# One more gate/up group ahead: TensorE's order in a fused cross-attention and mixture-of-experts kernel, lead of three against lead of four

## The chip, the cores and the metric

The kernel runs on one core of one Trainium2 chip. The metric is device time in microseconds (us); three runs of the kernel before stand below, and one further execution was profiled.

## The reference

Input `x` is 4 x 1024 tokens of width 256 in fp32, `ctx_1024` is 4 x 154 context rows of the same width.

```
x = x + attention(layernorm(x), ctx, ctx)        # one head, keys masked, softmax over 154 keys
xn = layernorm(x)                                # 4096 tokens
combine = top-8-of-16 routing weights of xn      # sigmoid scores, normalised, zero elsewhere
g, u = xn @ w_gate[e], xn @ w_up[e]              # 256 -> 128, for each of 16 experts
y[e] = (silu(g) * u) @ w_down[e]                 # 128 -> 256
x = x + sum_e combine[e] * y[e] + shared expert  # the shared one is expert 0 of the kernel's 17
```

## The kernel before

The 4096 tokens go in eight chunks of 512. For each chunk all 17 experts (`NE = 17`, numbered 0 to 16, number 0 the shared one) are computed, with all weights resident in SBUF as a high and a low part, so that each product is three matmuls. Chunks are indexed `(b, hf)`; a hardware loop `pe.Fori(0, B - 1)` of three turns holds two chunks per turn, and the last two chunks stand behind it. Every engine has its own copy of this loop.

One expert of one chunk takes these steps, each by the engine named:

- `gate_up(e)`, TensorE: six matmuls of 512 columns into `gate_ps[i]`, then six into `up_ps[i]`. There are two PSUM banks of each, `i` alternating from expert to expert.
- `tanh_gate(e)`, ScalarE (L666): tanh of the gate bank into `ew[i]`.
- `silu_up(e)`, VectorE: L949 combines tanh and the gate bank and signals `silu_done`; L953 multiplies by the up bank and signals `prod_done`.
- `weighted(e)`, GpSimd (L1160, L1153 for expert 0): times the token's routing weight, into `h[i]`.
- `hidden_hi(e)`, ScalarE (L673), and `hidden_lo(e)`, VectorE (L959): the high and low parts `hs[i]`. `hidden_hi(e)` waits for `down_done` of expert e - 2, whose `hs` it overwrites.
- `down(e)`, TensorE: twelve matmuls of 256 columns that accumulate into `y_ps`.

TensorE's order is written out by hand in `chunk`: at step s it issues `down(s)`, then pieces of work for the next chunk that are due at s (`front(s)`), then `gate_up(s + 3)`, then the pieces due at s + .5. `gate_up(e)` waits for `silu_done` of expert e - 2 ahead of its first matmul (its gate bank was read for the last time), and for `prod_done` of expert e - 2 ahead of its seventh. Numbers past 16 are experts of the next chunk, written 0', 1' and so on below.

The pieces for the next chunk are placed by tables. On TensorE: `turn_x` 2.5, `scores` 4.5 and 5.5, `turn_p` 7.5, `attend` 8.5, `turn_ln2` 11.5 (transposes of the second layernorm's output, L386, into `f_ps`), `logits` 12.5, `turn_z` 13, `turn_c` 15. VectorE's order at step s is `silu_up(s + 2)`, front(s), `hidden_lo(s + 1)`, front(s + .5); ScalarE's is `tanh_gate(s + 2)`, front(s), `hidden_hi(s + 1)`, front(s + .5); GpSimd's is `weighted(s + 1)`, front(s + .5). VectorE has at 9.5 the residual (L900), the statistics of the second layernorm (L823, L829), at 10.5 its scaling (L836), at 11.5 the low parts of its transposes (L854, after ScalarE's L617). All four engines take their instructions in this order and none is skipped over a wait.

Ahead of the loop TensorE runs the attention and routing of the first chunk, then `gate_up` 0, 1 and 2, while ScalarE and VectorE split the staged weights (`split_w`, L613 and L818).

Of the kernel before, what the change touches and what calls it, by code (L numbers as in the profile page):

```python
# [50 lines left out]
def xattn_moe_kernel(nc, x, ctx, mask, Wq, bq, Wk, bk, Wv, bv, gate_w, w_gate, w_up, w_down,  # L51
                     sw_gate, sw_up, sw_down, out):
    B, S, D = x.shape
    KEYS = ctx.shape[1]
    E, _, H = w_gate.shape
    TOK = 512
    TILES = TOK // P
    CHUNKS = B * S // TOK
    KD = D // P
    NE = E + 1  # L60
# [18 lines left out]
    with ExitStack() as stack:  # L79
# [101 lines left out]


        FREE = 2

        def upto(b, hf, per, k):

            return b * (2 * per) + (per * hf + k)

        def first_chunk(b, hf):
            return isinstance(b, int) and b == 0 and hf == 0  # L190

        def wait_apart(eng, *waits):


            counts = [n if isinstance(n, int) else eng.to_reg(n) for _, n in waits]
            eng.wait_ge(consts_set, 1)
            for (what, _), n in zip(waits, counts):
                eng.wait_ge(what, n)
# [5 lines left out]
        def slot(hf, e):  # L204

            return (NE * hf + e) % 2

        def nxt(hf, e):

            return (hf, e) if e < NE else (hf + 1, e - NE)  # L210
# [5 lines left out]
        def _(sp):  # L216
            sp.sem_inc(stored, 16 * FREE)
            sp.dma_start(ctx_in[:, 0:CT - 1, :], ctx_rows[0:(CT - 1) * P, :].rearrange("(t p) d -> p t d", p=P)) \
# [28 lines left out]
            def spread(b, hf, pair):  # L247

                stored_c = (c_stored, upto(b, hf, 16, 16))
                if pair >= PLACES:  # L250
                    wait_apart(sp, (h_done, upto(b, hf, NE, 2 * (pair - PLACES) + 3 + FREE)))
                elif first_chunk(b, hf):
                    wait_apart(sp, stored_c)
                else:
                    wait_apart(sp, (h_done, upto(b, hf - 1, NE, 2 * (pair + PLACES) + 3 + FREE)), stored_c)
                sp.dma_start(cb[:, pair % PLACES].rearrange("p a t -> p (a t)"),
                             c_rows[2 * pair:2 * pair + 2, :].rearrange("a t -> (a t)").partition_broadcast(P)) \
                    .then_inc(cb_loaded[pair % PLACES], 16)
# [4 lines left out]
            def chunk(b, hf, load):  # L263
# [5 lines left out]
                for pair in range(PLACES):  # L269
                    spread(b, hf + 1, pair)  # L270
                sp.wait_ge(y_added, upto(b, hf, 2, 2 + FREE))
                sp.dma_start(out_rows[b * 2 + hf], x2[:, hf]).then_inc(stored, 16)

            def last_stores():

                for q in range(2):
                    sp.wait_ge(y_added, 2 * CHUNKS + FREE - 1 + q)
                    sp.dma_start(out_rows[CHUNKS - 1, :, 2 * q:2 * q + 2, :], x2[:, 1, 2 * q:2 * q + 2, :]) \
                        .then_inc(stored, 16)
# [7 lines left out]
            last_stores()  # L287
            sp.wait_ge(stored, 16 * (CHUNKS + 1 + FREE))


        @block.tensor
        def _(pe):
            mm = nc.tensor.matmul

            def three_pass(ps, pairs, first, last):

                for i, ((lh, ll), (rh, rl)) in enumerate(pairs):
                    mm(ps, lh, rh, start=first and i == 0, stop=False)  # L298
                    mm(ps, lh, rl, start=False, stop=False)  # L299
                    ins = mm(ps, ll, rh, start=False, stop=last and i == len(pairs) - 1)  # L300
                return ins
# [151 lines left out]
            def turn_c(b, hf):  # L453
                pe.wait_ge(combined, upto(b, hf, 1, 1))
                for j in range(TILES):
                    ins = nc.tensor.transpose(f_ps[1][0:E, j * P:(j + 1) * P], cw[:, j, :], ident[:])
                ins.then_inc(c_turned, 1)

            def gate_up(b, hf, e):
                hf, e = nxt(hf, e)  # L460
                i, par = slot(hf, e), hf % 2
                if e == 0:
                    pe.wait_ge(t2_hi, upto(b, hf, 2, 2))
                    pe.wait_ge(t2_lo, upto(b, hf, 2, 2))
                if hf == 0:
                    pe.wait_ge(w_hi, e + 1)
                    pe.wait_ge(w_lo, e + 1)
                for ps, col, free, done in ((gate_ps, 0, silu_done, gate_done), (up_ps, UP0, prod_done, up_done)):
                    pe.wait_ge(free, upto(b, hf, NE, e - 1 + FREE))
                    ins = three_pass(ps[i][:], [((W[:, e, HI, col + k * H:col + (k + 1) * H],  # L470
                                                  W[:, e, LO, col + k * H:col + (k + 1) * H]),
                                                 (xT[:, par, HI, k, :], xT[:, par, LO, k, :])) for k in range(KD)],
                                     first=True, last=True)
                    ins.then_inc(done, 1)

            def down(b, hf, e):
                i = slot(hf, e)
                pe.wait_ge(h_hi, upto(b, hf, NE, e + 1 + FREE))
                pe.wait_ge(h_lo, upto(b, hf, NE, e + 1 + FREE))
                if e == 0:  # L480
                    pe.wait_ge(y_added, upto(b, hf, 2, FREE))
                for j in range(TILES):


                    c = slice(j * P, (j + 1) * P)
                    ins = three_pass(y_ps[j // 2][:, (j % 2) * D:(j % 2 + 1) * D],
                                     [((hs[:, i, HI, c], hs[:, i, LO, c]),
                                       (W[:, e, HI, DN0:DN0 + D], W[:, e, LO, DN0:DN0 + D]))],
                                     first=e == 0 and j % 2 == 0, last=e == NE - 1 and j % 2 == 1)
                    if e == NE - 1 and j == 1:  # L490
                        ins.then_inc(y_half, 1)
                ins.then_inc(down_done, 1)

            def front(at, b, hf):

                for part in due(PE_AT, "turn_x", at):
                    turn_x(b, hf, part)
                for part in due(PE_AT, "scores", at):
                    scores(b, hf, part)
                for part in due(PE_AT, "turn_p", at):  # L500
                    turn_p(b, hf, part)
                for part in due(PE_AT, "attend", at):
                    attend(b, hf, part)
                for part in due(PE_AT, "turn_ln2", at):
                    turn_ln2(b, hf, part)
                if due(PE_AT, "logits", at):
                    logits(b, hf)
                if due(PE_AT, "turn_z", at):
                    turn_z(b, hf)
                if due(PE_AT, "turn_c", at):  # L510
                    turn_c(b, hf)

            def chunk(b, hf, ahead, last):
                for s in range(NE):
                    down(b, hf, s)
                    if ahead:
                        front(s, b, hf + 1)
                    if s + 3 < NE or not last:
                        gate_up(b, hf, s + 3)
                    if ahead:  # L520
                        front(s + .5, b, hf + 1)

# [27 lines left out]
            pe.wait_ge(v_lo, 2 * B)  # L550
            gate_up(0, 0, 0)
            turn_c(0, 0)
            gate_up(0, 0, 1)
            gate_up(0, 0, 2)
            with pe.Fori(0, B - 1) as b:
                chunk(b, 0, True, False)
                chunk(b, 1, True, False)
            chunk(B - 1, 0, True, False)
            chunk(B - 1, 1, False, True)

# [658 lines left out]
```

## Time and profile before

| | us |
|---|---|
| three runs | 711.46, 715.76, 718.47 |
| median | 715.76 |
| span of the profiled execution | 717.8 |
| TensorE matmul busy in that span | 691.6 |
| VectorE, ScalarE, GpSimd busy | 459.2, 239.8, 260.7 |

The span runs from the first to the last instruction of the profiled execution. Nothing else was recorded of that execution's time: its span is 2.0 above the median of the three runs and inside their range. The page names TensorE "PE", VectorE "DVE", ScalarE "ACT", GpSimd "POOL". A matmul row's duration reaches past the start of the next one, since matmuls are pipelined, so the pace is read from starts.

### The profile page before, as it was taken

How to read it: one execution, taken by the hardware profiler on the slowest of the kernel's cores; microseconds unless marked ns; L12 is line 12 of the kernel's file. 1: busy time of each engine (PE TensorE's matmuls, PEld its weight loads, DVE VectorE, ACT ScalarE, POOL GpSimd, SP SyncE). 2: the span in 40 equal slices, each digit the busy share in tenths (PEclk: the TensorE clock that was granted, in tenths of full speed). 3: DMA queues.
4: the chain of work that ended last, by engine and by line, in shares of the span. 5: the costliest groups of instructions: out<-in, count | busy, mean ns of one | idle time of the engine just before them, and what ended most of it. 6: DMA issues, size and time to landing. Idle time of an engine off the chain costs nothing.

```text
span 717.8 us, 11775 instructions
## 1 busy us (share of the span) xinstructions
PE 691.6 (96%) x3995; PEld 595.8 (83%) x3995; DVE 459.2 (64%) x1029; ACT 239.8 (33%) x485; POOL 260.7 (36%) x222
## 2 busy tenths in 40 slices
PE   7997799999999899999999899999999999999997
PEld 6575688888888788888888788888988888888886
DVE  4576666677667475777566576677565775775444
ACT  4345233333424134233333234242334233232221
POOL 2120432535343242435344243434324343433432
PEclk9799999999999899999999999999999999999999
DMA  6315511032110510005100411005110421006100
GB/s 184 111 32 162 184 60 46 13 103 106 59 31 1 180 60 30 30 24 185 59 30 1 151 59 60 30 2 192 46 58 0 136 94 38 1 3 204 61 0 31
DMA packets 32772, 51.30 MB, mean 71 GB/s; under 512 B 3918, under 2 KB 24391, under 8 KB 32711
## 3 DMA queue, kind: packets, MB, share of 16 engines
q1 hardware_dynamic: 32455, 50.23, 21.6%
q8 instruction: 37, 0.61, 0.4%
q10 hardware_dynamic: 256, 0.26, 0.2%
q14 instruction: 24, 0.20, 0.1%
HBM read 46.03 MB, written 4.46 MB: 70 GB/s over the span
## 4 chain that ended last, share of the span: by engine, by line
PE 91%; issue 4%; DVE 2%; POOL 1%; ACT 1%; DMA 1%; POOLq 0%; SPq 0%; DVEq 0%; ACTq 0%
PE y_ps L298 9%; PE y_ps L300 9%; PE y_ps L299 9%; PE gate_ps L298 9%; PE up_ps L298 9%; PE gate_ps L300 9%; PE gate_ps L299 8%; PE up_ps L300 8%; PE up_ps L299 8%; PE f_ps L386 2%; PE f_ps L408 2%; PE f_ps L419 1%; PE up_ps L368 1%; PE up_ps L307 1%; DMA xin<-in_x_dram 1%
## 5 line engine op out<-in xcount | busy, mean ns | idle before, releaser
L1160 POOL TENSOR_TENSOR hidden<-hidden,cb 128x512 f32<-128x512 f32 x128 | 200.1, 1565 | 308.2 <-DVE hidden L953 257.4
L949 DVE SCALAR_TENSOR_TENSOR hidden<-hidden,gate_ps 128x512 f32<-128x512 f32 x136 | 93.2, 685 | 156.2 <-ACT hidden L666 145.9
L666 ACT ACTIVATE hidden<-gate_ps 128x512 f32<-128x512 f32 x136 | 81.5, 599 | 275.0 <-PE gate_ps L300 273.4
L298 PE MATMUL y_ps<-W,hs 128*128 128x256 f32 x544 | 157.9, 290 | 13.4 <-issue 5.7
L300 PE MATMUL y_ps<-W,hs 128*128 128x256 f32 x544 | 154.8, 284 | 0.0
L299 PE MATMUL y_ps<-W,hs 128*128 128x256 f32 x544 | 154.5, 284 | 0.0
L298 PEld LDWEIGHTS y_ps<-W,hs 128*128 128x128 f32 x544 | 103.8, 191 | 19.9 <-issue 9.5
L959 DVE TENSOR_TENSOR hs<-hidden,hs 128x512 fp32r<-128x512 f32 x136 | 95.6, 703 | 29.1 <-ACT hs L673 29.1
L298 PE MATMUL gate_ps<-xT,W 128*128 128x512 f32 x272 | 109.1, 401 | 0.0
L298 PE MATMUL up_ps<-xT,W 128*128 128x512 f32 x272 | 108.8, 400 | 0.0
L300 PE MATMUL gate_ps<-xT,W 128*128 128x512 f32 x272 | 108.2, 398 | 0.0
L299 PE MATMUL gate_ps<-xT,W 128*128 128x512 f32 x272 | 107.8, 396 | 0.0
L299 PE MATMUL up_ps<-xT,W 128*128 128x512 f32 x272 | 107.6, 396 | 0.0
L300 PE MATMUL up_ps<-xT,W 128*128 128x512 f32 x272 | 107.5, 395 | 0.0
L299 PEld LDWEIGHTS y_ps<-W,hs 128*128 128x128 f32 x544 | 103.9, 191 | 3.9
L953 DVE TENSOR_TENSOR hidden<-hidden,up_ps 128x512 f32<-128x512 f32 x136 | 93.6, 688 | 16.6 <-PE up_ps L300 1.9
L300 PEld LDWEIGHTS y_ps<-W,hs 128*128 128x128 f32 x544 | 103.9, 191 | 0.0
L673 ACT ACTIVATE hs<-hidden 128x512 fp32r<-128x512 f32 x136 | 85.2, 626 | 47.2 <-POOL hidden L1160 47.2
L300 PEld LDWEIGHTS up_ps<-xT,W 128*128 128x128 f32 x272 | 51.6, 190 | 12.8
L299 PEld LDWEIGHTS up_ps<-xT,W 128*128 128x128 f32 x272 | 52.0, 191 | 12.0
L298 PEld LDWEIGHTS up_ps<-xT,W 128*128 128x128 f32 x272 | 51.5, 189 | 12.1
L300 PEld LDWEIGHTS gate_ps<-xT,W 128*128 128x128 f32 x272 | 51.7, 190 | 11.6
(141 smaller groups left out, 726.3 us busy)
## 6 DMA issues: line engine op xcount, KB each, us to landing
cb<-c_rows SPq DMA_DIRECT2D x64, 512.0 KB, 4.2
xin<-in_x_dram SPq DMA_DIRECT2D x8, 512.0 KB, 3.8
out_dram<-x SPq DMA_DIRECT2D x7, 512.0 KB, 7.4
stage<-in_L_ffn_w_gate_dram SPq DMA_DIRECT2D x16, 128.0 KB, 2.3
stage<-in_L_ffn_w_up_dram SPq DMA_DIRECT2D x16, 128.0 KB, 2.5
stage<-in_L_ffn_w_down_dram SPq DMA_DIRECT2D x16, 128.0 KB, 2.6
cb<-in_ctx_dram SPq DMA_DIRECT2D x1, 512.0 KB
out_dram<-x SPq DMA_DIRECT2D x2, 256.0 KB, 2.1
```

Source lines behind the costliest of these rows:

```text
L298: mm(ps, lh, rh, start=first and i == 0, stop=False)
L299: mm(ps, lh, rl, start=False, stop=False)
L300: ins = mm(ps, ll, rh, start=False, stop=last and i == len(pairs) - 1)
L307: nc.tensor.transpose(up_ps[0][:, 0:P], ident[:], ident[:])
L386: ins = nc.tensor.transpose(f_ps[k][:, j * P:(j + 1) * P], xn[:, j, k * P:(k + 1) * P], ident[:])
L408: mm(to[:, 0:2 * KEYS], xT[:, par, HI, k, c], A[:, bi, k].rearrange("p s q -> p (s q)"), start=k == 0, stop=False)
L666: af(ew[:, i, :], gate_ps[i][:], ACT.Tanh, scale=0.5).then_inc(tanh_done, 1)
L673: af(hs[:, i, HI, :], h[:, i, :], ACT.Copy).then_inc(h_hi, 1)
L949: V_.scalar_tensor_tensor(out=ew[:, i, :], in0=ew[:, i, :], scalar=1.0, in1=gate_ps[i][:], op0=ALU.add, op1=ALU.mult).then_inc(silu_done, 1)
L953: V_.tensor_tensor(ew[:, i, :], ew[:, i, :], up_ps[i][:], ALU.mult).then_inc(prod_done, 1)
L959: V_.tensor_tensor(hs[:, i, LO, :], h[:, i, :], hs[:, i, HI, :].bitcast(F32), ALU.subtract) \
L1160: pg.tensor_tensor(h[:, i, :], ew[:, i, :], cb[:, pair % PLACES, (e - 1) % 2, :], ALU.mult) \
```

## The change

TensorE's `gate_up` runs four ahead of `down` in place of three; the groups ahead of the loop become four. The other engines' orders, the placing tables, the buffers and their number, and the waits in `gate_up` and `down` stay.

```diff
         FREE = 2
+        LEAD = 4
...
                     down(b, hf, s)
                     if ahead:
                         front(s, b, hf + 1)
-                    if s + 3 < NE or not last:
-                        gate_up(b, hf, s + 3)
+                    if s + LEAD < NE or not last:
+                        gate_up(b, hf, s + LEAD)
                     if ahead:
                         front(s + .5, b, hf + 1)
...
             gate_up(0, 0, 0)
             turn_c(0, 0)
-            gate_up(0, 0, 1)
-            gate_up(0, 0, 2)
+            for e in range(1, LEAD):
+                gate_up(0, 0, e)
```

## Rows read from the trace of the kernel before

**Rows 1.** The page: busy time of each engine and its share of the span.

```profile
PE 691.6 (96%) x3995; PEld 595.8 (83%) x3995; DVE 459.2 (64%) x1029; ACT 239.8 (33%) x485; POOL 260.7 (36%) x222
```

**Rows 2.** The view of waits for TensorE: released by whom, us, times, longest.

```profile
PE y_ps L298 <- issue: 5.7, 2, 3.1
PE y_ps L298 <- ACT hs L673: 4.6, 1, 4.6
PE y_ps L298 <- DVE hs L959: 3.0, 2, 2.2
```

**Rows 3.** Timeline of TensorE in the second chunk, slot 10 to slot 11: start, duration.

```profile
207.73 0.39 PE L298 MATMUL gate_ps<-xT,W 128*128 128x512 f32 x1
...
210.51 0.28 PE L298 MATMUL y_ps<-W,hs 128*128 128x256 f32 x1
...
211.94 0.39 PE L298 MATMUL gate_ps<-xT,W 128*128 128x512 f32 x1
```

**Rows 4.** Timeline of VectorE in the same stretch.

```profile
205.73 0.69 DVE L949 SCALAR_TENSOR_TENSOR hidden<-hidden,gate_ps 128x512 f32<-128x512 f32 x1 [0.51 <-ACT hidden L666]
208.62 0.69 DVE L959 TENSOR_TENSOR hs<-hidden,hs 128x512 fp32r<-128x512 f32 x1 [1.37 <-ACT hs L673]
209.24 2.38 DVE L836 TENSOR_SCALAR xn<-x,meanvar,small 128x256 f32<-128x256 f32 x4
211.54 0.67 DVE L949 SCALAR_TENSOR_TENSOR hidden<-hidden,gate_ps 128x512 f32<-128x512 f32 x1
```

**Rows 5.** Timeline of the same chunk around `turn_ln2` and step 12.

```profile
214.73 1.04 PE L386 MATMUL f_ps<-ident,xn 128*128 128x128 f32 x8
216.00 1.29 DVE L854 TENSOR_TENSOR xT<-f_ps,xT 128x512 fp32r<-128x512 f32 x2 [2.46 <-ACT xT L617]
217.03 0.39 PE L298 MATMUL gate_ps<-xT,W 128*128 128x512 f32 x1
217.21 0.68 DVE L949 SCALAR_TENSOR_TENSOR hidden<-hidden,gate_ps 128x512 f32<-128x512 f32 x1
```

**Rows 6.** Timeline at the same step of the seventh chunk, the last of seven with such a front.

```profile
628.06 0.39 PE L298 MATMUL gate_ps<-xT,W 128*128 128x512 f32 x1
628.24 0.68 DVE L949 SCALAR_TENSOR_TENSOR hidden<-hidden,gate_ps 128x512 f32<-128x512 f32 x1
```

**Rows 7.** Timeline at the loop's start: silu 2, low part 1 and `down(1)`.

```profile
74.73 0.68 DVE L949 SCALAR_TENSOR_TENSOR hidden<-hidden,gate_ps 128x512 f32<-128x512 f32 x1
80.04 1.00 DVE L959 TENSOR_TENSOR hs<-hidden,hs 128x512 fp32r<-128x512 f32 x1 [3.91 <-ACT hs L673]
81.18 0.55 PE L298 MATMUL y_ps<-W,hs 128*128 128x256 f32 x1 [4.56 <-ACT hs L673]
```

**Rows 8.** Timeline after the second return of the loop: silu 2' and slot 0.

```profile
408.53 0.69 DVE L949 SCALAR_TENSOR_TENSOR hidden<-hidden,gate_ps 128x512 f32<-128x512 f32 x1 [5.03 <-issue]
...
409.99 0.63 PE L298 MATMUL gate_ps<-xT,W 128*128 128x512 f32 x1
```

**Rows 9.** Timeline of the last chunk's end.

```profile
701.62 0.39 PE L298 MATMUL gate_ps<-xT,W 128*128 128x512 f32 x1
...
704.40 0.28 PE L298 MATMUL y_ps<-W,hs 128*128 128x256 f32 x1
...
712.01 0.69 DVE L959 TENSOR_TENSOR hs<-hidden,hs 128x512 fp32r<-128x512 f32 x1 [1.84 <-ACT hs L673]
712.85 0.36 PE L298 MATMUL y_ps<-W,hs 128*128 128x256 f32 x1 [0.87 <-DVE hs L959]
```

**Rows 10.** Windows: PE, PEld, DVE, ACT, POOL busy, then granted clock, DMA share, GB/s.

```profile
24.00:25.00 1.00, 0.00 (x0) 0.00 (x0) 1.00 (x3) 0.97 (x4) 0.00 (x0) 1.00 0.74 223
27.00:36.00 9.00, 9.00 (x24) 4.90 (x23) 3.04 (x13) 1.93 (x7) 0.00 (x0) 0.50 0.18 53
70.00:74.00 4.00, 1.85 (x14) 1.81 (x15) 2.62 (x4) 2.71 (x5) 0.00 (x0) 1.00 0.77 200
81.00:84.00 3.00, 2.82 (x13) 2.85 (x14) 2.97 (x8) 0.15 (x1) 2.85 (x2) 0.50 0.45 180
```

## Prediction

> **What bounds the kernel now.** I read the page first, then TensorE's waits, then the timeline step by step. TensorE is busy 96% of the span, the next engine 64% [rows 1], so a TensorE stall anywhere lengthens the kernel and an earlier result elsewhere is worth nothing by itself. Its waits are few [rows 2]: 5.7 us at two returns of the hardware loop with "issue" as releaser (no data was awaited), 4.6 us once and 3.0 us in two pieces for `hs`, that is for `down`. These 7.6 us are all that a longer lead over `down` can address. In between TensorE runs without a gap: slot 10 starts at 207.73, `down(11)` at 210.51, slot 11 at 211.94 [rows 3]. So `gate_up` takes 2.78 us, `down` 1.43, a plain step 4.21.
>
> **What the edit moves.** The number of instructions stays. In steady state the time at which `down(s)` and each front piece starts is set by the work ahead of them. I measure everything from these: keep the times of `down` and of the fronts, and the edit puts `gate_up(s + 4)` into the very slot in which `gate_up(s + 3)` stood. Each gate/up group thus comes 4.2 us earlier against its own `down`, and the extra group is issued once, ahead of the loop. Slot 11, after `down(11)`, starts at 211.94 [rows 3]: it held `gate_up(14)`, which needs silu 12, and will hold `gate_up(15)`, which needs silu 13. So each slot now asks for a VectorE result that is one expert younger. The waits to go through are those for `silu_done(s + 2)` in slot s, and for `prod_done(s + 2)` 1.39 us later. I compared this slot by slot with the present times of VectorE. In plain steps silu s + 2 ends 1.3 us ahead of the slot (silu 12 at 205.73 + 0.69 = 206.42 against slot 10 at 207.73 [rows 3, 4]) and would end earlier still, as its gate group comes earlier. The exceptions are slots 11 and 12, and they repeat in each of the seven chunks that carry a front.
>
> **Slot 11.** Silu 13 (L949) runs 211.54 to 212.21 [rows 4], 0.27 us after the slot's start at 211.94 [rows 3]. Can it move up? It is queued on VectorE behind the scaling L836 (2.38 us from 209.24), and that behind `hidden_lo(11)` at 208.62, which ScalarE releases [rows 4]; ScalarE waits for GpSimd's `weighted(11)`, GpSimd has its layernorm piece of 9.5 ahead of that, and the piece waits for VectorE's statistics of the residual. So the chain hangs on TensorE's `attend`, whose time I hold fixed. Only the start of the residual can move, since `hidden_lo(10)` gets out of its way; its second half needs the second half of `attend`, so I take 0.12 off. From a VectorE end to a released matmul it is 0.14 us at `down(1)` (80.04 + 1.00 to 81.18) [rows 7] and 0.15 at the last `down` (712.01 + 0.69 to 712.85) [rows 9]; I take 0.15. The stall is 0.27 - 0.12 + 0.15 = 0.30 us. A released matmul with nothing in flight also starts its group late: 0.36 for the first matmul of the last `down` against 0.28 [rows 3, 9], 0.1 more. Slot 11 costs 0.40 us; bounds 0 (if the chain moves up by 0.5) and 0.6.
>
> **Slot 12.** It comes right after `turn_ln2` and `down(12)`, and `gate_up(16)` needs silu 14. VectorE has the two low parts L854 ahead of that silu, released by ScalarE's high parts, which wait for `turn_ln2`. From 214.73, where `turn_ln2` starts, silu 14 ends at 217.21 + 0.68 = 217.89, 3.16 us later; the slot starts at 217.03, 2.30 us later [rows 5]. L854's two fill 216.00 to 217.29, so all of it is back to back and starts at a TensorE instruction, so no earlier gate group shortens it: 3.16 + 0.15 - 2.30 = 1.01 us, plus 0.10 for the empty pipeline, 1.1 us; bounds 1.0 and 1.25. The seventh chunk shows the same distance: slot 628.06, silu to 628.24 + 0.68 = 628.92, so 0.86 late as in the second [rows 5, 6], and so do the five others. The up half of the slot is then no limit, as its product is ready 0.7 us after the silu and the bank is wanted 1.4 us after. Queued behind the waiting gate group are `logits`, `down(13)` and all that follows, so both stalls go into the total. Slots 11 and 12 together: 1.5 us a chunk, times 7 = +10.5 us; bounds 7.0 and 13.
>
> The Trainium skill, page "Perfetto Trace Analysis", section "Optimization Strategy", says that the same gap repeating on the engine that should be saturated can mean too little SBUF or PSUM for the next tile. By that rule a deeper order over the same two banks brings gaps; the distance in [rows 5] is where it would show.
>
> **Ahead of the loop.** TensorE now waits 2.2 us ahead of the first `down` [rows 2] and 4.56 us ahead of the second [rows 7]. `gate_up(3)` fills the first gap: it needs silu and product of expert 1, which VectorE's order has ahead of the low part that `down(0)` waits for. `gate_up(4)` then waits for silu 2, which ends at 75.41 [rows 7], and is over at about 78.3. The second `down` cannot start before its low part ends at 81.04, which waits for the routing weights, so it starts at 81.18 as now. Nothing is gained by that time except that one group more is behind us: the 2.78 us are paid out at the other end. The half clock that follows the second gap, 0.50 in 81 to 84 [rows 10], I leave as it is, since a gap of 2.9 us remains; at full clock 1.5 us would be gained.
>
> **Loop returns.** The fetch that shows as "issue" follows the same instruction in the same slot. After it slot 0 asks for silu 2' where VectorE itself has just come back: it ends at 409.22 against a slot at 409.99 [rows 8], 0.8 us early, and earlier in the other return. Cost nil. The cover is the half clock that runs there; at full clock `down(0)` would be over some 0.8 us sooner and the slot would wait 0.2 us.
>
> **The end.** Slot 12 of the last chunk, at 701.62, takes the last group. Then come `down` 13 to 16 with nothing between. `down(13)` starts at 704.40 [rows 9] and is through at about 706.0; `hidden_hi(15)` and `hidden_lo(15)`, which wait for its buffer, take some 0.7 us each (0.69 for L959) and with the hand-overs let `down(15)` start at 707.5, 0.3 late; the same for `down(16)`, which starts at about 709.05. Now it starts at 712.85, after 0.87 us of waiting [rows 9]. Gain 3.8 us, of which 2.8 are the group paid out and 1.0 the stalls gone; bounds 3.3 and 4.1.
>
> **Sum.** +10.5 - 3.8 = +6.7 us, so the profiled span goes from 717.8 to 724.5. Against the median of 715.76 that is 722.4. The span of 717.8 lies inside the three runs, so I carry the difference over unscaled.
>
> **Rivals.**
> (a) No stall in slots 11 and 12, only the end's gain: 715.8 - 3.8 = 712.0. For it: every wait for data in [rows 2] is for `down`, and the chains of slots 11 and 12 contain engines that are half idle. Against it: in slot 12 nothing idles between `turn_ln2` and silu 14. The same time would come if the lead existed in the order only and the two `hs` buffers held it back. Chance 12%.
> (b) Clearly slower: the two stalls, some 1.5 us within 6 us, cost TensorE its full clock in each chunk. One short gap (no matmul in 24 to 25) was followed by a granted clock of 0.50 from 27 to 36. Against it: the 2.2 us gap between 70 and 74 left it at 1.00 [rows 10]. One such stretch cost 1.5 us after 81.18, where `down` and `gate_up` ran at 0.50 for 3 us [rows 10], half of that lost. Seven of them: 722.4 + 7 x 1.5 = 732.9. It decides from the point where a 1.1 us wait within dense matmuls is enough for a drop to 1.2 GHz. Chance 12%.
> The Trainium skill, page "TensorE: Matmul & The Clock Gate", section "A second HAM failure mode: psum-queue depth-cycling", has this case: a kernel that cycles PSUM banks idles briefly between groups and its clock swings. By that page the time would be that of (b).
> (c) The stalls are right but smaller, with the second gap before the loop no longer lowering the clock: 7.0 - 3.8 - 1.5 = +1.7, 717.5. It is the lower edge of my own case.
>
> **How the numbers follow.** The forecast case holds 76%, (a) and (b) 12% each. Its own range is 717.5 to 725.0 (13 - 3.8 = +9.2), and the median of three or so runs moves by 2 us. To hold 8 in 10 I reach down to 713, most of the way to (a), and up to 729, into a case (b) with a drop in some chunks. A measurement of this kernel can tell about 1% from no change. One per cent slower is 722.9, just above the forecast, that is at 1.57 us a chunk: 40% of the forecast case and all of (b) make 0.42. One per cent faster is 708.6, which no case reaches: 0.03. The rest, 0.55, is within 1%.
>
> **What would show it.** In the changed profile TensorE's waits should have a new entry of about 14 gate matmuls (L298, `gate_ps`) released by VectorE's L949, 9 to 10 us in total, longest about 1.1, in slots 11 and 12 of seven chunks. The wait for the second `down` should shrink from 4.6 to about 2.9. The last `down` should follow the last gate group by some 7.4 us in place of 7.0 us, with three `down` groups between them in place of two. If slot 12 shows no gap, the fixed-frame argument is wrong. The prediction fails upwards if windows of granted clock 0.50 turn up in the middle of chunks, and downwards if the front's VectorE work starts earlier than `attend` and `turn_ln2` allow now.

## The result, and the profile after

| | before | lead of four |
|---|---|---|
| median of 20 runs each, us | 715.32 (710.95 to 721.49) | 719.98 (717.29 to 728.14) |
| ratio, 95% interval | | 1.0088 (1.006 to 1.0116) |
| span of the profiled execution | 717.8 | 726.3 |

The kernel is slower by 0.9%, 6.3 us by the ratio and 4.7 us by the two medians; 722.4 was forecast. The profiled execution of the changed kernel is its slowest run (728.14 us), in a slower state of the chip that the ratio leaves out. So spans are not compared below, but places inside them. The profile of before starts its first gate/up group at 56.32, this one at 59.57; from that start to the last matmul's it is 657.9 us before and 663.2 after, +5.3 us. (All line numbers past 184 are one higher in the changed kernel; those of the experiments shift by a few more.)

The page's busy line, set against [rows 1], tells nothing: TensorE's share is 96% in both kernels. The view of waits for TensorE in the changed kernel tells more, set against [rows 2]:

```profile
PE gate_ps L299 <- DVE hidden L950: 6.8, 8, 1.5
PE y_ps L299 <- issue: 6.2, 2, 3.2
PE y_ps L299 <- ACT hs L674: 3.1, 1, 3.1
...
PE y_ps L299 <- DVE hs L960: 0.2, 1, 0.2
```

A new releaser stands first: VectorE's silu, eight times. One of the eight is ahead of the loop (1.5 us), the other seven are slot 12 of the seven chunks with a front, 0.75 to 0.85 each. The waits for `down` shrank from 7.6 us to 3.3. So the lead does what it is meant to do, and hands more than that to another wait.

The timeline of the second chunk in the changed kernel, slots 11 and 12, answers to [rows 4, 5]:

```profile
215.97 0.28 PE L299 MATMUL y_ps<-W,hs 128*128 128x256 f32 x1
...
216.87 0.68 DVE L950 SCALAR_TENSOR_TENSOR hidden<-hidden,gate_ps 128x512 f32<-128x512 f32 x1
...
217.60 0.50 PE L299 MATMUL gate_ps<-xT,W 128*128 128x512 f32 x1
...
220.49 1.04 PE L387 MATMUL f_ps<-ident,xn 128*128 128x128 f32 x8
...
221.28 0.36 PE L299 MATMUL y_ps<-W,hs 128*128 128x256 f32 x1
...
221.76 1.29 DVE L855 TENSOR_TENSOR xT<-f_ps,xT 128x512 fp32r<-128x512 f32 x2 [2.89 <-ACT xT L618]
...
222.96 0.68 DVE L950 SCALAR_TENSOR_TENSOR hidden<-hidden,gate_ps 128x512 f32<-128x512 f32 x1
...
223.69 0.50 PE L299 MATMUL gate_ps<-xT,W 128*128 128x512 f32 x1 [0.75 <-DVE hidden L950]
```

Slot 11 would start at 215.97 + 1.43 = 217.40; silu 13 ends at 217.55 and the gate group starts at 217.60. It carries no mark of a wait, because the duration given for the row before it runs on past the next start and covers the gap: such waits are seen only by comparing starts. Slot 12 would start at 221.28 + 1.50 = 222.78; silu 14 ends at 223.64, the group starts at 223.69, 0.91 us late, though the view counts 0.75. Both groups begin with 0.50 in place of 0.39. `down(11)` to `down(12)` takes 5.31 us (5.02 before), `down(12)` to `down(13)` 6.23 (5.21 before): 1.3 us a chunk. All other steps of this chunk are those of before to 0.1 us.

The end of the changed kernel, against [rows 9]:

```profile
714.01 0.39 PE L299 MATMUL gate_ps<-xT,W 128*128 128x512 f32 x1
...
716.80 0.28 PE L299 MATMUL y_ps<-W,hs 128*128 128x256 f32 x1
...
719.98 0.36 PE L299 MATMUL y_ps<-W,hs 128*128 128x256 f32 x1 [0.18 <-DVE hs L960]
...
721.48 0.28 PE L299 MATMUL y_ps<-W,hs 128*128 128x256 f32 x1
```

The last chunk takes 59.45 us from its first to its last `down`, 63.21 before: 3.76 us less.

### The profile page after: what moved, and what is told of

Same layout as the page of the kernel before. It is cut to its first block, busy times and chain, and to the rows that moved or that the text cites. A ratio compares the mean times of both kernels' runs of the same rounds, so it can differ in the third digit from the quotient of the medians.

```text
span 726.3 us, 11775 instructions
## 1 busy us (share of the span) xinstructions
PE 697.9 (96%) x3995; PEld 597.4 (82%) x3995; DVE 466.4 (64%) x1029; ACT 238.7 (33%) x485; POOL 248.8 (34%) x222
## 4 chain that ended last, share of the span: by engine, by line
PE 80%; DVE 9%; issue 5%; ACT 2%; POOL 2%; DMA 1%; SPq 0%; POOLq 0%; ACTq 0%; DVEq 0%
PE gate_ps L299 8%; PE gate_ps L301 8%; PE up_ps L299 8%; PE gate_ps L300 8%; PE up_ps L300 7%; PE up_ps L301 7%; PE y_ps L299 7%; PE y_ps L301 7%; PE y_ps L300 7%; DVE xn L837 2%; POOL hidden L1161 2%; PE f_ps L387 2%; PE f_ps L409 2%; DVE x L901 1%; DVE stats L824 1%
## 5 line engine op out<-in xcount | busy, mean ns | idle before, releaser
L1161 POOL TENSOR_TENSOR hidden<-hidden,cb 128x512 f32<-128x512 f32 x128 | 188.8, 1477 | 302.3 <-DVE hidden L954 246.3
L960 DVE TENSOR_TENSOR hs<-hidden,hs 128x512 fp32r<-128x512 f32 x136 | 103.5, 761 | 81.9 <-ACT hs L674 81.9
```

The source lines that it names most:

```text
L960: V_.tensor_tensor(hs[:, i, LO, :], h[:, i, :], hs[:, i, HI, :].bitcast(F32), ALU.subtract) \
L1161: pg.tensor_tensor(h[:, i, :], ew[:, i, :], cb[:, pair % PLACES, (e - 1) % 2, :], ALU.mult) \
```

## The experiments

The theory (queue theory in the expectations): VectorE takes its work in order, a lead of four asks for a silu that stands behind pieces of the next chunk's layernorm, and TensorE waits in slots 11 and 12 for that alone. The first rival (buffer theory): a deeper order over the same two banks and two `hs` buffers costs by itself, wherever the pieces stand. Each ratio is against runs of the kernel before in the same session and on the same chip. The rows come from several sessions on different chips, so two rows' ratios compare less surely than either with 1; rows of one run have no interval. In the table a "chunk" is the distance from the first `down` of the sixth chunk to that of the seventh, the first that neither a loop return nor its aftermath touches; steps 11 and 12 are `down` to `down` in the second chunk, and the last chunk is first to last `down`. All are differences of starts in the timeline of TensorE.

| run | ratio (95% interval) | median | chunk | step 11 | step 12 | last chunk |
|---|---|---|---|---|---|---|
| before | 1 | 715.3 | 80.07 | 5.02 | 5.21 | 63.21 |
| lead of four | 1.0088 (1.006 to 1.0116) | 720.0 | 81.39 | 5.31 | 6.23 | 59.45 |
| l4_both | 0.9975 (0.9942 to 1.0007) | 711.9 | 80.09 | 5.02 | 5.21 | 59.44 |
| l3_both | 0.9981 (0.9946 to 1.0016) | 713.6 | 80.07 | 5.01 | 5.21 | 63.21 |
| l4_turn11 | 1.0004 (0.9972 to 1.0036) | 713.3 | 80.06 | 5.07 | 5.17 | 59.45 |
| l4_t2 | 1.0008 (0.9977 to 1.0038) | 714.1 | 80.37 | 5.31 | 5.22 | 59.44 |
| l4_scale | one run | 716.2 | 81.08 | 5.02 | 6.22 | 59.44 |
| l4_extra | 1.0316 (1.024 to 1.0393) | 735.7 | 84.14 | 5.31 | 8.99 | 59.45 |
| l3_extra | 1.0017 (0.9976 to 1.0058) | 715.2 | 80.04 | 5.01 | 5.21 | 63.20 |
| l4_last3 | one run | 728.7 | 81.37 | 5.31 | 6.24 | 61.76 |
| l3_last4 | one run | 713.1 | 80.07 | 5.01 | 5.22 | 62.23 |
| l3_unroll | 0.9912 (0.9873 to 0.9952) | 709.5 | 80.07 | 5.01 | 5.21 | 63.21 |
| l4_unroll | 0.9971 (0.9932 to 1.0011) | 714.1 | 81.38 | 5.31 | 6.23 | 59.44 |
| l4_turn11_unroll | 0.9804 (0.9739 to 0.987) | 701.7 | 80.06 | 5.07 | 5.17 | 59.45 |

**Both pieces out of the way: l4_both.**

```diff
-            ... t2_hi=(11.5, 11.5)         # ScalarE
+            ... t2_hi=(12, 12)
-            ... ln2_scale=(10.5, 10.5), t2_lo=(11.5, 11.5)      # VectorE
+            ... ln2_scale=(11, 11), t2_lo=(12, 12)
```

> Lead of four; ScalarE's and VectorE's pieces of the second layernorm's transposes (L617, L854) moved from 11.5 to 12, VectorE's scaling from 10.5 to 11, so that silu 13 and silu 14 stand ahead of them in VectorE's queue. Queue theory (the loss is VectorE's order: the awaited silu stands behind front pieces): no TensorE wait for a silu in slots 11 and 12, the chunk interval back from 81.4 to 80.1 us, the total 3.8 us under the kernel before, ratio about 0.995. Rival, buffer theory (the two hs buffers and the busier VectorE cost the time, wherever the pieces stand): chunk interval stays near 81.4, ratio near 1.009.

Both waits are gone and the chunk is back at 80.09 us. The timeline of VectorE in that kernel shows the new order: silu 13 ahead of the scaling, silu 14 ahead of the low parts.

```profile
206.28 0.68 DVE L950 SCALAR_TENSOR_TENSOR hidden<-hidden,gate_ps 128x512 f32<-128x512 f32 x1
...
207.60 3.02 DVE L837 TENSOR_SCALAR xn<-x,meanvar,small 128x256 f32<-128x256 f32 x4
...
211.14 0.68 DVE L950 SCALAR_TENSOR_TENSOR hidden<-hidden,gate_ps 128x512 f32<-128x512 f32 x1
...
213.18 1.29 DVE L855 TENSOR_TENSOR xT<-f_ps,xT 128x512 fp32r<-128x512 f32 x2 [0.64 <-ACT xT L618]
```

Against the changed kernel this is 1.1% less (0.9975 to 1.0088). The buffer theory falls, since banks, buffers and all work are the same. That doesn't mean that the number of banks plays no part: what the gate group waits for is its bank, which the silu reads last. Whether a third gate bank would remove the waits too was not run. Against the kernel before, the expected 0.995 lies in the interval, but so does no change.

**The control: l3_both**, the same two moves with a lead of three.

> Lead of three with the same two moves; the control. Queue theory: slots 11 and 12 ask for silu 12 and 13, which were in time already, so nothing changes: chunk interval 80.1, ratio 1.000 within 0.3%. If moving the pieces is worth something by itself (rival to the reading of the run above), this one is faster too, ratio about 0.987 if it is worth the 1.3 us a chunk.

Chunk, steps and last chunk are those of before to 0.02 us, and the ratio does not differ from 1. The moves are worth nothing where slots 11 and 12 ask for silu 12 and 13.

**TensorE's order alone: l4_turn11.**

```diff
-PE_AT = dict(... turn_ln2=(11.5, 11.5),
+PE_AT = dict(... turn_ln2=(11, 11),
```

> Lead of four, and only TensorE's order changed: turn_ln2 at 11 in place of 11.5, that is ahead of gate group 15 instead of behind it. The other engines' orders stay. Queue theory: the transposes can start 2.8 us earlier against slot 12 (the scaled input is ready 0.3 us before), so silu 14 is ready about 1.9 us ahead of slot 12, and silu 13 is ready 0.5 us ahead of slot 11, which now starts 0.8 us later: both waits vanish, interval 80.1, ratio about 0.995. Buffer theory: TensorE's order of the transposes is no matter, ratio near 1.009.

One entry of TensorE's table removes both waits, with the other engines as they were. The timeline of that kernel, second chunk:

```profile
210.05 0.67 DVE L950 SCALAR_TENSOR_TENSOR hidden<-hidden,gate_ps 128x512 f32<-128x512 f32 x1
...
210.57 1.03 PE L387 MATMUL f_ps<-ident,xn 128*128 128x128 f32 x8
...
211.96 1.28 DVE L855 TENSOR_TENSOR xT<-f_ps,xT 128x512 fp32r<-128x512 f32 x2
213.16 0.68 DVE L950 SCALAR_TENSOR_TENSOR hidden<-hidden,gate_ps 128x512 f32<-128x512 f32 x1
```

Silu 14 now ends at 213.84; slot 12 starts at 215.66, so it is 1.8 us early (1.9 expected). Silu 14 needs nothing of `turn_ln2`; it only stands behind its low parts in VectorE's queue. Putting gate group 15 between the transposes and slot 12 gives VectorE the 2.8 us to get through them. The ratio, 1.0004 (0.9972 to 1.0036), is 0.8% below the changed kernel's, but the expected 0.995 lies outside its interval. In this kernel's profile the way from the first gate group to the last matmul is 651.0 us, 6.9 less than before (657.9), so why its runs don't show the end's gain stays open.

**One part each: l4_t2** (only L618 and L855 at 12) **and l4_scale** (only L837 at 11).

> Lead of four, and only the pieces L617 and L854 moved from 11.5 to 12; the scaling stays at 10.5. Queue theory: slot 12 no longer waits (it cost 0.9 to 1.0 us a chunk), slot 11 still waits 0.2 us; interval 80.3 to 80.4, ratio about 0.998. Buffer theory: ratio near 1.009.

> Lead of four, and only VectorE's scaling of the second layernorm moved from 10.5 to 11, behind silu 13. Queue theory: slot 11 no longer waits (step 11 from 5.31 to 5.01 us), slot 12 still does (step 12 stays 6.2), interval about 81.1.

Each removes the wait it was expected to and leaves the other: l4_t2 has steps of 5.31 and 5.22 us, l4_scale 5.02 and 6.22. Their savings, 1.02 and 0.31 us against the changed kernel's 81.39, are together 1.33; l4_both saves 1.30. So the two waits are separate, and slot 12 carries three quarters.

**More of it: l4_extra and l3_extra**, two VectorE operations that only write a scratch buffer.

```diff
+                if at == 11.5:
+                    for i in range(2):
+                        w0 = W[:, 0, HI, 0:TOK].bitcast(F32)
+                        V_.tensor_tensor(spare[:, i, :], w0, w0, ALU.subtract)
```

> Lead of four, with two added VectorE operations (128 x 512, SBUF to a scratch buffer that nothing reads, about 0.65 us each) behind L854 at 11.5, ahead of silu 14 in VectorE's queue. Queue theory: TensorE's wait in slot 12 grows by what they take, 1.3 us: step 12 from 6.2 to 7.5 us, interval from 81.4 to 82.7, ratio about 1.022. Buffer theory (total VectorE work counts, at 64% busy): 1.3 us of work in an 80 us chunk is absorbed, ratio stays at 1.009.

> Lead of three with the same two operations at the same place. Queue theory: slot 12 asks for silu 13, which is ahead of them, and silu 14 has 3 us to spare before slot 13, so nothing changes: step 12 stays 5.2 us, ratio 1.000. If added VectorE work costs wherever it stands (rival), both leads slow down by the same 1.3 us a chunk.

The same 1.28 us of VectorE work costs nothing that the runs can tell at a lead of three (1.0017, 0.9976 to 1.0058), and 2.3% at a lead of four (1.0316 against 1.0088, where 1.022 was expected). That settles that the queue ahead of silu 14 is what TensorE waits for, not VectorE's total. But the cost is more than the 1.2 us a chunk by which the wait grew. Step 12 is 7.43 to 7.50 us in three of the seven chunks, as expected, and 8.98 to 8.99 in the four others. Windows of this kernel show why: busy of PE, PEld, DVE, ACT, POOL, granted clock, DMA share, GB/s, first after the wait of the second chunk, then after that of the third.

```profile
218.00:219.00 1.00, 1.00 (x5) 0.83 (x6) 1.00 (x2) 0.00 (x0) 0.30 (x1) 1.00 0.00 0
219.00:222.00 3.00, 3.00 (x9) 2.35 (x8) 1.51 (x3) 0.00 (x0) 2.64 (x2) 0.53 0.00 0
...
306.00:309.00 3.00, 3.00 (x15) 2.08 (x14) 1.90 (x4) 0.00 (x0) 2.67 (x2) 1.00 0.00 0
```

After the same wait, 2.11 us from start to start (the view counts 1.95), TensorE's clock fell to 1.2 GHz in the one chunk (0.53) and stayed at 2.4 GHz in the other (1.00). The drop costs 8.99 - 7.43 = 1.6 us. A longer wait doesn't decide it alone: the seventh chunk's is 2.21 us and its clock stays at 1.00. That is the prediction's rival (b), not in the changed kernel, where the waits in slot 12 are 0.91 to 1.00 us and the granted clock is 1.00 behind all seven, but one step beyond.

**Where the end's gain comes from: l4_last3 and l3_last4.** The edit of l4_last3, whose last chunk has a lead of three and no group in slot 0, is below. l3_last4 is the opposite: a lead of three, and in the last chunk two groups in slot 0 and a lead of four.

```diff
-                    if s + LEAD < NE or not last:
-                        gate_up(b, hf, s + LEAD)
+                    lead = 3 if last else LEAD
+                    if (s + lead < NE or not last) and not (last and s == 0):
+                        gate_up(b, hf, s + lead)
```

> Lead of four up to the last chunk, which issues no gate/up group in slot 0 and runs with a lead of three. If the end's gain is the group issued ahead of the loop, paid out when the groups run out (my sum), 2.8 us of it stay whatever the last chunk's order, and only the stalls ahead of the last two down groups come back (0.9 and 0.1 in place of 0.2): last chunk 60.4 us from its first to its last down, against 59.45 with a lead of four and 63.2 before. Rival: the whole 3.8 us come from the lead within the last chunk; then 63.2.

> Lead of three up to the last chunk, which issues gate/up groups 3 and 4 in slot 0 and runs with a lead of four. Seven chunks as before (interval 80.07, no wait in slots 11 and 12). Queue theory with the group count as in my sum: the last chunk has one group more to do than with a lead of four throughout and one as before, and only the waits ahead of its last down groups shrink, from 0.87 and 0.12 to about 0.2: last chunk 62.4 us against 63.2 before. Rival: the lead within the last chunk gives the whole 3.8 us; then 59.45.

l4_last3's last chunk is 61.76 us, 1.4 more than expected, but far from 63.2. The missing piece is a wait for the second `down`'s input that I had not seen, 1.22 us from start to start (1.07 in the view): with slot 0 empty it comes 2.8 us sooner, and the low part of expert 1, which waits for the routing weights, is not there yet. The waits ahead of the last two `down` groups are 0.12 and 0.87 us, as in the kernel before. l3_last4 has 62.23 us against 62.4 expected, with one wait of 0.18 us. So of the 3.76 us, 63.21 - 62.23 = 0.98 are the waits at the end, and 62.23 - 59.45 = 2.78 are one gate/up group less to do in the last chunk, issued where TensorE had waited ahead of the loop.

**The loop, and the fastest kernel: l3_unroll, l4_unroll, l4_turn11_unroll.** The hardware loops of all engines are written out:

```diff
-            with pe.Fori(0, B - 1) as b:
+            for b in range(B - 1):
```

> The kernel before with its hardware loops written out, on all engines. The two waits marked issue at the returns (5.7 us) and the half clock behind them (1 to 3 us each) should go: 8 to 11 us less, ratio about 0.987. Rival: instruction fetch of the longer program costs as much elsewhere, ratio 1.00.

> Lead of four, loops written out. Queue theory: the two waits in slots 11 and 12 have nothing to do with the loop, so the distance to the kernel with a lead of three and loops written out is that of the looped pair, +5 to +7 us: ratio to the kernel before about 0.995. Rival: part of the loss comes from the loop's returns (VectorE comes back late and slot 0 asks for its silu); then the two written-out kernels are closer than 4 us.

> Lead of four, turn_ln2 at 11, loops written out: 3 to 4 us below the lead of three with loops written out, ratio about 0.982, the fastest of all. If the lead's gain depends on the loop, equal to it.

Both waits marked "issue" at the returns are gone, and in l3_unroll every chunk after the first takes 80.1 us, where the kernel before had 81.7 to 83.4 in those up to the fifth. The lead of four behaves in it as in the loop (81.4 to 81.8 us in six intervals). The two written-out kernels are a factor of 1.006 apart (0.9971 to 0.9912). That is 4.6 us by the medians, as the looped pair's 4.7, and 5.7 by the two profiles from the first gate group to the last matmul (651.9 and 646.2). So the return is no part of the lead's loss that these runs can tell. With `turn_ln2` at 11 the written-out kernel takes 701.7 us, 2.0% under the kernel before (1.3% to 2.6% by the interval) and the fastest of all.

Two expectations were off. l4_turn11_unroll is 7.8 us below l3_unroll by the medians, where 3 to 4 were expected; in the profiles it is 4.5 us (641.7 against 646.2 from the first gate group to the last matmul), and the rest is not explained. And l3_unroll's 0.9912 (0.9873 at the best edge) is short of 0.987, 6.1 us by the medians, though in its profile the same way is 11.7 us shorter than before (646.2 against 657.9). Most of that difference is the choice of executions: l3_unroll's profile is its fastest run of twelve (705.6, median 709.5), and that of before, at a time of about 719.6 us by my estimate (span 717.8, and every run recorded with both takes 1.8 to 1.9 us more than its span), is 4.3 above its median.

## Why the prediction was right

**The frame.** The step that carried it was to hold the times of `down` and the fronts and to ask, slot by slot, whether a silu one expert younger is there. Slots 11 and 12 were named from the profile of before and are the only ones in which the changed kernel waits for a silu inside a chunk. l4_both, l4_t2, l4_scale and l4_turn11 each remove what they should.

**Slot 12.** Forecast 1.1 us, measured 1.02 (6.23 - 5.21) in the second chunk. Silu 14 ends 223.64 - 220.49 = 3.15 us after the start of `turn_ln2`, 3.16 before. The hand-over from VectorE's end to TensorE's start was 0.05 us, not the 0.15 taken from the two released `down` groups.

**Slot 11.** Forecast 0.40, measured 0.29 (5.31 - 5.02). Silu 13 moved up against `down(11)` by (212.21 - 210.51) - (217.55 - 215.97) = 0.12 us, as taken; the hand-over was again 0.05.

**The sum of the stalls.** 7 x 1.5 = 10.5 was forecast. Measured are 1.31 us in six chunks and 1.4 in the seventh, 9.3 together (the two undisturbed distances between chunks give 1.32 and 1.44: 81.39 and 81.51 against 80.07). The term mis-sized is the hand-over: it is 0.05 us in six chunks, where 0.15 was taken, and twelve times 0.10 is the 1.2 us missing. In the seventh chunk, the one with a front that stands behind the loop, it is 0.15 us in both slots, and there the forecast of 0.40 and 1.1 is met (steps of 5.38 and 6.31). Its slot 12:

```profile
639.56 0.68 DVE L950 SCALAR_TENSOR_TENSOR hidden<-hidden,gate_ps 128x512 f32<-128x512 f32 x1
...
640.39 0.47 PE L299 MATMUL gate_ps<-xT,W 128*128 128x512 f32 x1 [0.85 <-DVE hidden L950]
```

In l4_unroll the hand-over in slot 12 is 0.15 in the first, third, fifth and seventh chunk and 0.05 in the others. What sets it was not tested.

**Ahead of the loop.** `gate_up(3)` filled the first gap, `gate_up(4)` waited 1.5 us for silu 2, and the second `down` waits for its input as before. The timeline of the changed kernel, to be held against [rows 7]:

```profile
78.95 0.50 PE L299 MATMUL gate_ps<-xT,W 128*128 128x512 f32 x1 [1.48 <-DVE hidden L950]
...
83.97 1.00 DVE L960 TENSOR_TENSOR hs<-hidden,hs 128x512 fp32r<-128x512 f32 x1 [4.36 <-ACT hs L674]
...
85.12 0.36 PE L299 MATMUL y_ps<-W,hs 128*128 128x256 f32 x1 [3.12 <-ACT hs L674]
```

The remaining gap is 3.1 us, 2.9 forecast. The clock still falls after it, as left in the sum (granted clock 0.50 from 88.5 to 89.5).

**The end.** Forecast 3.8, measured 3.76. From the last gate group to the last `down` it is 721.48 - 714.01 = 7.47 us, forecast 7.4.

**The sum.** -3.8 + 9.3 = +5.5 us by the profile, +6.7 forecast, +6.3 by the ratio (4.3 to 8.3), +4.7 by the medians. The comparison doesn't resolve the 1.2 us between the first two, so that the ratio lies nearer the forecast than the profile does is luck. One reading in the sum was wrong without harm: it held the span of 717.8 against the times of three runs. By the same estimate of 1.8 us between span and time that execution took about 719.6 us, above all three (718.47). The forecast only carried the difference over to the median, so it does not change.

**What I said the profile would show** was right in kind and wrong in count: fourteen waits of 9 to 10 us in all, where the view lists seven inside the chunks with 5.3 us. The view counts from the end of the row before, which lies 0.16 us past the next start in this kernel, and leaves out the late first matmul; so slot 11's waits of 0.20 us don't appear in it, and slot 12's 0.91 appear as 0.75.

**The rivals.** (a), no stall, falls by the timeline. (b), the half clock, did not come at waits of 0.9 to 1.0 us; l4_extra shows that it does at 2.11, in four chunks of seven. At the prediction's price of 1.5 us a chunk it would have made the changed kernel some 10 us slower than it is. The Trainium skill tells of a kernel that cycles PSUM banks and whose clock swings ("TensorE: Matmul & The Clock Gate", "A second HAM failure mode: psum-queue depth-cycling"); this trace does not show that, its window of 224 to 230 has a granted clock of 1.00. The Trainium skill's remark that a repeating gap can mean too little PSUM ("Perfetto Trace Analysis", "Optimization Strategy") agrees with the look of the gap, and what is waited for is a bank; but l4_turn11 removes the gap with the same banks.

## What to carry to other kernels

When a producer is let run further ahead, look up for every slot what the group that moves into it waits for, in the timeline that you have, and with it everything that stands ahead of that result in its engine's queue; a half idle engine can still be late with one item. A longer lead pays only up to the point where its wait reaches past a piece that hangs on TensorE's own later work, and then one entry in the order of that work (here the transposes ahead of the gate group) can remove the wait without another buffer. Count gaps from start to start: a view of waits hides those shorter than the overlap of two rows.

## What the runs showed of the hardware that was not expected

- The clock after one and the same wait: in l4_extra waits of 2.11 us within dense matmuls were followed by a granted clock of 1.2 GHz in four chunks and not in two, nor was one of 2.21. Waits of 0.91 to 1.00 us were followed by it in none of seven chunks of the changed kernel.
- A return of the hardware loop costs more than its gap of 2.6 to 3.2 us. In the profile of before, the second to fifth chunk, with both returns among them, take 331.0 us together, in l3_unroll 320.4: 10.6 more, of which 5.7 are the two gaps. The granted clock is half from 241 to 248 and from 408 to 412. The amount differs from run to run: in l3_extra it is 7.6 in place of 10.6.
- A gate matmul released by VectorE started 0.05 us after the silu's end in the first six chunks of the changed kernel and 0.15 in the seventh; a `down` matmul started 0.14 or 0.15 us after the low part's end.
- The first gate/up group started between 52.2 us (l3_extra) and 60.1 us (l3_both) in the profiles, with nothing changed ahead of it. This and the clock after the returns are as large as the effect studied, so the effect can be read from inside the trace more surely than from a few runs.
